# A four-layer graph network on one core: layers 2 and 3 aggregate x before the product with W, two tiles further behind, and the attention output stored as two halves

## The reference

```python
x = _layernorm(x + _L0_gnn_ref(x, adj, L0_gnn_W, L0_gnn_b), axis=-1)
x = _layernorm(x + _L1_gnn_ref(x, adj, L1_gnn_W_heads, ...), axis=-1)
x = _layernorm(x + _L2_gnn_ref(x, adj, L2_gnn_W, L2_gnn_a_src, L2_gnn_a_dst), axis=-1)
x = _layernorm(x + _L3_gnn_ref(x, adj, L3_gnn_W, L3_gnn_a_src, L3_gnn_a_dst), axis=-1)
```

```python
Wh = jnp.einsum('bnd,de->bne', x, W)
...
attn = jax.nn.softmax(logits, axis=-1)
...
out = jnp.einsum('bnm,bmd->bnd', attn, Wh)
```

## Time and profile before

| | |
|---|---|
| median of 3 runs | 3347.15 us (3345.89 to 3349.83) |
| the profiled execution's own time | 3340.33 us |
| its span, first to last instruction | 3338.6 us |
| mean granted TensorE clock | 0.986 of full speed |
| busy share of the span | PE 96%, DVE 71%, POOL 60%, ACT 50% |
| stage 2, 1000 to 1400 us: PE busy | 399.04 of 400 us |
| stage 3, 19 steps from 2411.05 to 2714.54 us: PE busy | 292.92 of 303.49 us |

### The profile page before, as it was taken

One profiled execution on the slowest core, in us unless ns is written; L12 is line 12 of the kernel. 1 busy time (PEld: TensorE's weight loads), 2 busy tenths in 40 slices (PEclk: granted clock), 3 DMA queues, 4 the chain that ended last, 5 costly groups with the idle time before them and its releaser, 6 DMA issues. The chain is left out here.

```text
span 3338.6 us, 63568 instructions
## 1 busy us (share of the span) xinstructions
PE 3211.0 (96%) x19033; PEld 2685.1 (80%) x19033; DVE 2372.1 (71%) x4961; ACT 1667.3 (50%) x4113; POOL 1990.1 (60%) x2861
## 2 busy tenths in 40 slices
PE   8999969999999999999999999997999999999997
PEld 6777748888889888988989899885777777777775
DVE  6777655676766676767676766746777777777875
ACT  2111125555555555555555555534666666656665
POOL 4555545545555455545454545404888888888886
PEclk9999989999999999999999999998999999999998
DMA  4343310000100100000000000002111111111110
GB/s 142 120 126 120 98 59 26 26 31 25 31 28 28 31 25 31 28 28 31 25 31 31 25 31 25 29 26 95 48 48 48 56 47 47 47 55 48 47 47 29
DMA packets 85613, 160.69 MB, mean 48 GB/s; under 512 B 9648, under 2 KB 9648, under 8 KB 85552
## 3 DMA queue, kind: packets, MB, share of 16 engines
q1 hardware_dynamic: 82992, 151.59, 13.8%
q0 software_dynamic: 2560, 8.39, 0.9%
HBM read 109.61 MB, written 50.33 MB: 48 GB/s over the span
## 5 line engine op out<-in xcount | busy, mean ns | idle before, releaser
L841 POOL TENSOR_TENSOR w_first<-xd,v_row 128x512 f32<-128x512 f32 x504 | 690.9, 1379 | 629.5 <-DMA xd<-x_scratch 333.0
L1191 PE MATMUL hp<-yT_hi,big_hi 128*128 128x256 f32 x2048 | 594.7, 290 | 0.3 <-DVE yT_lo L1055 0.3
L1191 PE MATMUL hp<-yT_hi,big_lo 128*128 128x256 f32 x2048 | 579.7, 283 | 0.0
L1191 PE MATMUL hp<-yT_lo,big_hi 128*128 128x256 f32 x2048 | 579.6, 283 | 0.0
L1205 PE MATMUL wop<-big_hi,hT_hi 128*128 128x512 f32 x1024 | 424.1, 414 | 0.0
L1205 PE MATMUL wop<-big_hi,hT_lo 128*128 128x512 f32 x1024 | 401.9, 392 | 0.0
L1205 PE MATMUL wop<-big_lo,hT_hi 128*128 128x512 f32 x1024 | 400.4, 391 | 0.0
L1191 PEld LDWEIGHTS hp<-yT_hi,big_hi 128*128 128x128 f32 x2048 | 392.7, 192 | 7.7 <-DVE yT_lo L1055 1.0
L1191 PEld LDWEIGHTS hp<-yT_lo,big_hi 128*128 128x128 f32 x2048 | 392.9, 192 | 2.8
L1191 PEld LDWEIGHTS hp<-yT_hi,big_lo 128*128 128x128 f32 x2048 | 392.8, 192 | 0.0
L890 ACT ACTIVATE w_first<-w_first 128x512 f32<-128x512 f32 x504 | 316.7, 628 | 134.4 <-POOL w_first L841 133.7
(11 more groups left out here) (198 smaller groups left out, 8052.1 us busy)
## 6 DMA issues: line engine op xcount, KB each, us to landing
xt<-in_x SPq DMA_DIRECT2D x64, 256.0 KB, 2.8
x_scratch<-x SPq DMA_DIRECT2D x64, 256.0 KB, 2.0
xa<-x_scratch SPq DMA_DIRECT2D x64, 256.0 KB, 2.7
att_scratch<-attT SPq DMA_DIRECT2D x64, 256.0 KB, 2.0
att<-att_scratch SPq DMA_DIRECT2D x64, 256.0 KB, 2.7
x1r<-x_scratch SPq DMA_DIRECT2D x64, 256.0 KB, 2.9
out<-res SPq DMA_DIRECT2D x64, 256.0 KB, 2.0
xd<-x_scratch SPq DMA_DIRECT2D x63, 256.0 KB, 2.7
```

The costliest lines, as they stand in the source:

```text
L841: nc.gpsimd.tensor_tensor(terms[:, k % TR, :], xd[:], v_row[:, k, :], ALU.mult).then_inc(terms_ready, 1)
L1191: ins = nc.tensor.matmul(hp[half][:, s * 2 * P:(s + 1) * 2 * P], a, b, start=c == 0 and i == 0, stop=c == KC - 1 and i == 2)
```

## The change

Layers 2 and 3 now multiply x with the probabilities first (`aggregate`: four float32 matmuls of 128 x 128, whose result comes out transposed), ACT and DVE split that into `aggS`, and the product with W goes straight into the bank `sums` that the residual reads. Both `turn_x`, `wh` and its copy, and `bank_a` are gone; each layer has a bank for its small results of its own. Layer 2's project follows one step after its aggregate, layer 3 stands two tiles further back (lags 3 to 6), and a project is issued in two halves with other work between. The pipeline ends after T + 6 steps, not T + 4. In stage 2 the attention output is split before it is stored: ACT makes the high part in `att_hi` (which also serves as `junk`), POOL the low part in `who`, and POOL then adds b2 in `attT`; three stores replace one, and three loads one in stage 3. There ACT copies the turned output (`att_n`) instead of DVE's addition of b2, and POOL's `att_lo` is gone; the probabilities are made by one ACT instruction, not by two of POOL; `gate` is applied as a scalar.

```diff
@@ stage 2, SP
+                sp.dma_start(b2_col[:], b2.rearrange("(c p) -> p c", p=P), allow_slow_non_contiguous=True).then_inc(b2_loaded, 16)
...
-                def store(s):
-                    sp.wait_ge(att_ready, s + 1)
+                def store(s, j):
+                    sp.wait_ge(att_hi_made, s + 1)
+                    sp.dma_start(rows(att_hi_rows, s), att_hi[:].bitcast(F32)).then_inc(att_hi_stored, 16)
+                    sp.wait_ge(att_lo_made, s + 1)
+                    sp.dma_start(rows(att_lo_rows, s), who[j][:]).then_inc(att_lo_stored, 16)
+                    sp.wait_ge(att_b2_made, s + 1)
                     sp.dma_start(rows(att_rows, s), attT[:]).then_inc(att_stored, 16)
@@ stage 2, POOL
+                def split_att(s, j):
+                    pool.wait_ge(att_hi_made, s + 1)
+                    nc.gpsimd.tensor_tensor(who[j][:].bitcast(F32R), attT[:], att_hi[:].bitcast(F32), ALU.subtract
+                                            ).then_inc(att_lo_made, 1)
...
+                    pool.wait_ge(att_lo_made, s + 1)
+                    nc.gpsimd.tensor_tensor(attT[:].rearrange("p (c n) -> p c n", c=KC),
+                                            attT[:].rearrange("p (c n) -> p c n", c=KC),
+                                            b2_col[:, :, None].to_broadcast([P, KC, P]), ALU.add
+                                            ).then_inc(att_b2_made, 1)
@@ stage 2, ACT
                     act.wait_ge(wo_done, 8 * m + 8)
-                    ge(act, uo_done, 2 * (m - 1) + j + 1)
+                    ge(act, att_lo_stored, 16 * (2 * (m - 1) + j + 1))
                     nc.scalar.copy(who[j][:], wop[j][:]).then_inc(who_ready, 1)
...
+                def split_att(s, pairs_done):
+                    act.wait_ge(att_ready, s + 1)
+                    act.wait_ge(ao_.f_ready, 2 * pairs_done)
+                    ge(act, att_hi_stored, 16 * s)
+                    nc.scalar.copy(att_hi[:], attT[:]).then_inc(att_hi_made, 1)
@@ stage 2, DVE, out_f
+                    ge(dve, att_hi_stored, 16 * (s - j))
+                    ge(dve, att_lo_made, s - j)
@@ stage 3, ACT
+                def prob(g, t):
+                    act.wait_ge(g.att.gated, t + 1)
+                    ge(act, g.att.turned_done, t)
+                    nc.scalar.activation(g.att.prob[:, 0, :, :],
+                                         g.att.ex[:, 0, None, :].to_broadcast([P, 2, NODES]),
+                                         ACT.Identity, scale=g.att.inv[:]).then_inc(g.att.prob_ready, 1)
@@ stage 3, PE
-                def turn_x(g, t, x, ready):
-                    pe.wait_ge(ready, t + 1)
-                    ge(pe, g.xT_lo_ready, t)
+                def aggregate(g, t, x):
+                    pe.wait_ge(g.att.turned_ready, 2 * t + 2)
+                    ge(pe, g.agg_lo_ready, t)
                     for c in range(KC):
...
+                        ins = nc.tensor.matmul(g.agg[:, c, :], x[:, c * P:(c + 1) * P], g.att.turned[:, 0, :],
+                                               start=True, stop=True)
+                    ins.then_inc(g.agg_done, 1)
+
+                def project(g, t, part):
+                    if part == 0:
+                        pe.wait_ge(g.agg_lo_ready, t + 1)
+                        ge(pe, g.z_ready, t)
...
+                    ins = product(nc, g.sums[:], g.aggS, (w_hi, w_lo),
+                                  [(c, g.q + c) for c in range(2 * part, 2 * part + 2)],
+                                  first=part == 0, last=part == 1)
...
-                def sums(g, t):
-                    pe.wait_ge(g.att.turned_ready, 2 * t + 2)
-                    pe.wait_ge(g.wh_ready, t + 1)
```

More of the change, by code:

```diff
@@ L942, in step @@
                         dots(*d1, (2,))
+                    if pair(p - 2):
+                        split_att(2 * (p - 2) + 1, p - 1)
                     if pair(p):
@@ L1393, in run @@
                         step(n + r, r)
-                for n in range(stop * R, T + 4):
+                for n in range(stop * R, T + 6):
                     step(n, n % R)
@@ L1492, in step @@
                                                 ).then_inc(x1b_ready, 1)
-                att_lo(0, 0)
-                run(pool, step, ahead=1)
+                    if live(n, 3):
+                        g2.norm.pool_rstd(nc, pool, n - 3, g2.x_ready, norm_consts)
+                    if live(n, 1):
+                        for k in range(2):
+                            terms(g2, n - 1, k, x2[(r - 1) % R][:], x2_ready)
+                        diag(g2, n - 1)
+                    if live(n, 3):
+                        for k in range(2):
+                            terms(g3, n - 3, k, x3[(r - 3) % R][:], g2.x_ready)
@@ L1497, in _ @@
+                run(pool, step)
             @block.scalar
             def _(act):
-                def att_hi(t, r):
-                    act.wait_ge(att_loaded[r % 2], pair(t, r))
-                    ge(act, h1_done, t - 1)
-                    nc.scalar.copy(attS[r % 2][0][:].rearrange("p c n -> p (c n)"), att[r % 2][:]
-                                   ).then_inc(att_hi_ready, 1)
-                def x_hi(g, t):
-                    act.wait_ge(g.xT_done, t + 1)
-                    ge(act, g.wh_done, t)
-                    nc.scalar.copy(g.xT[0][:], g.turn[:]).then_inc(g.xT_hi_ready, 1)
@@ L1584, in _ @@
                 weights_hi(0)
-                att_hi(0, 0)
                 weights_hi(1)
-                run(act, step, ahead=1, behind=behind)
+                run(act, step, behind=behind)
             @block.vector
@@ L1728, in project @@
-                def project(g, t):
-                    pe.wait_ge(g.xT_lo_ready, t + 1)
-                    if isinstance(t, int) and t == 0:
-                        pe.wait_ge(w_lo_parts, g.q + KC)
-                    product(nc, bank_a[:], g.xT, (w_hi, w_lo),
-                            [(c, g.q + c) for c in range(KC)]).then_inc(g.wh_done, 1)
+                        ins = nc.tensor.matmul(g.agg[:, c, :], x[:, c * P:(c + 1) * P], g.att.turned[:, 0, :],
+                                               start=True, stop=True)
@@ L1767, in step @@
                         ins.then_inc(att_turned, 1)
-                        pe.wait_ge(att_lo_ready, n + 1)
+                    if live(n, 3):
+                        project(g2, n - 3, 0)
+                    if live(n, 2):
+                        spread(g2, n - 2)
+                    if live(n, 5):
+                        aggregate(g3, n - 5, x3[(r - 5) % R])
+                    if live(n, 3):
+                        project(g2, n - 3, 1)
+                    if live(n, 4):
+                        spread(g3, n - 4)
+                    if live(n, 0):
+                        pe.wait_ge(attS_loaded[r % 2], twice(n, r))
                         ge(pe, y_ready, n)
@@ L1803, in step @@
                                 ).then_inc(y_done, 1)
-                    if live(n, 2):
-                        sums(g2, n - 2)
+                    if live(n, 4):
+                        g3.att.pe_turn(nc, pe, n - 4, ident)
                 def behind(g, k):
```

352 lines of the change are left out of this document (164 added, 188 removed).

## The result

The changed kernel takes 3250.88 us (3248.71 to 3252.24, four runs), the kernel before 3346.52 us beside it. The ratio is 0.9716, 95% interval 0.9699 to 0.9733: faster by 95.6 us. The profiled executions differ less: 3340.33 before, 3252.24 after, their spans 3338.6 and 3250.3 us, so 88.3 us between the spans.

A forecast was written before the change was run, and what follows sets the result against it. The prediction took PE as the bound throughout. Its terms, -76.6 + 1 + 6.3 - 1 + 0 = -70.3 us, took the profiled 3340.33 to 3270; 6.8 up to the median gave 3277 us, range 3255 to 3318.

The forecast's parts named there:

- Term 1: Stage 3's 62 steps between the w2 products of tiles 1 and 63: from 15.94 to 14.70 us each, -76.6 us.
- The 0.1 for waits: Stage 3: allowance of 0.1 us a step for small PE waits, raising the step from 14.60 to 14.70 us.
- The margin of 0.6 us at h1: Stage 3: DVE's copy of h1 is there at 8.1 us, PE's transposes of it come at 8.7.
- The one ahead of the w2 product: Stage 3: margin with `h1T_lo` ready by 10.8 us and the w2 product at 11.5.
- Term 2: Stage 2's loop: new waits and POOL work cost +1 us for the whole stage (0 to +5).
- The three new waits: Stage 2: the next load of `xd`, the output's next exp and `keep_wo` wait on new work or stores; priced within +1 us.
- Terms 3, 4 and 5: End of stage 2, +6.3 us; stage 3's first product, -1 (-3 to +2); drain, 0 (-4 to +8).
- The step from the profiled time to the median: Whole kernel before: the profiled execution of 3340.33 us lies 6.8 below the median of 3347.15, so 3270 becomes 3277.
- The second: Stage 3: aggregates at 0.81 us and no wait, a step of 14.44, 3261 us, or 3250 with shorter drain; chance 0.08.
- The first: Stage 3: DVE late for h1 again, 15.3 to 15.4 us a step, about 3317 us; chance 0.21.
- The third and fourth: Stage 2: PE waits for a bank, 3341 or 3373 us, 0.07; stage 3: DVE-POOL chain, 15.9 a step, 3347, 0.04.

The follow-up runs named there:

- the doubled transposes: The kernel before with gate as a scalar and layer 2's four transposes of x issued twice in stage 3: 3321.15 us, ratio 0.9935.

## Why the prediction was wrong in size

**Bound and direction** held: PE is the bound of stage 3, and no gap is to be seen in its steps now.

**Term 1, "15.42 - 0.86 - 1.74 + 1.78 = 14.60" and 14.70 with waits**: this is the step that failed. The steady step took 14.38 us, and the 62 steps came out 25.2 us below the term. The reading that failed most is the 15.42 it starts from. Its parts:
- The start, "PE works 15.42", was busy time. The work was 15.20 (shown by the doubled transposes): 0.22 a step, 14 us. PE lost 0.77 us a step to waits, and the list of waits showed 0.55. The sign stood in the earlier trace rows: between 2720.84 and 2722.05 lie 1.21 us for two groups of four transposes, of which I took each for 0.43, and of the 0.35 that is left only 0.18 is listed.
- The aggregates take 0.81 and 0.87, 1.68 and not 1.78: 6 us.
- The 0.1 for waits was not needed: 6 us. The margin of 0.6 us at h1 is there: DVE's copy ran from 2617.12 to 2617.81 and the transposes start at 2618.41. The one ahead of the w2 product is as small (`h1T_lo` ends at 2620.45, the product starts at 2621.05).
- Against these stands what is left over, 0.1 us a step, 6 us. It is the balance of small slots: one of the removed groups of transposes took 0.35 and not 0.43, and each transpose of the probabilities takes 0.11 (2618.30 to 2618.41) where the timeline before has 0.03, while the transposes of h1 take 0.35 for 0.43. These add up to 0.16; the 0.06 beyond 0.10 is within what the rounding of that many slots can make.
- The first steps of the pipeline, with layer 3 two tiles further behind, take 9.89, 12.12 and 13.22 us; I counted 62 full ones: 5 us.

Of the 1.60 us by which a step got shorter, 0.42 goes with `gate` alone (shown); 0.35 is a wait for `xT_lo` that appears in its place as soon as `gate` holds nothing up (shown); and 0.82 is work of PE. In most steps before, the 0.77 us of waits all stood ahead of `turn_h`.

**Term 2, "+1 us for the whole of stage 2"**: 5.7 in this pair of profiles, by the tie. The three new waits that I priced do not reach PE; the eight profiles together show no cost of the change in the loop. Two numbers there were also wrong: a pair is 39.5 + 14.8 = 54.3 us long, not 48.5, which only leaves DVE more room, and POOL's first product, 5 us later than 1531.24, would come at 1536.2 and not 1536.6.

**Terms 3, 4 and 5** held: +6.2 for +6.3, -0.9 for -1, -0.3 for 0. Term 3 held by its chain; in terms 4 and 5 the sums alone are confirmed, and there is luck in term 4: inside it the first product comes 0.7 us later behind the loads, not earlier, and the steps behind it make up 1.6.

**The step from the profiled time to the median**, +6.8 us, was the second error. The profiled execution of before had its first output sum 2.0 to 2.6 us earlier than the three versions of it; what else made it 6.8 us faster than the median isn't shown (its 9 long pairs are near the average). That of after, with 21 long pairs, lay 1.4 us above its own median. That is 8.2 us of the 26 between forecast and result.

**Rivals.** The second, "more than forecast", came closest (aggregates at 0.81, no wait: 14.44 and 3261), but it too started from 15.42. The first, DVE late for h1 again, is ruled out by the changed kernel and stays away even with `gate` as a product of two tensors. The third and fourth did not happen.

## What to carry to other kernels

Work of an engine is read between starts, in a step that doesn't wait, and summed; a busy share with modelled ends can hide short waits, here 0.22 us a step before and 0.35 in the version with `gate` as a scalar. Where PE's rows list no wait, those of its weight loads can. Before a median is forecast from one profiled run, count in it what comes and goes (here pairs with and without a tie). Where an edit takes a wait away, look for a second edit that does so too: by themselves they seem to be worth the same microseconds twice.

## Unexpected

- 0.02 us decide 0.5: which of POOL's 128 x 512 product and DVE's `hT_lo` starts first changes the latter from 0.69 to 1.82 us. The profiles have 5 to 21 long pairs, so it moves stage 2 by some 8 us from run to run; 28 x 0.5 = 14 us would be the most, by this estimate.
- Four float32 matmuls of 128 columns in a row cost 0.81 to 0.87 us and four transposes 0.35 to 0.44, by what stands beside them: the same aggregate takes 0.87 behind a spread and 0.81 behind the transposes that were added there.
- One tensor operand less freed DVE from POOL: 1.10 us fell to 0.21 for the same 128 x 1 result.
